# Second attention of a gated cross-attention stack: TensorE turns two heads and then scores two heads, where it did one of each in turn

## The chip, the cores and the metric

The kernel runs on one core of one Trainium2 chip. The metric is device time of one execution in microseconds (us); the time of a kernel is the median of several executions. The profile is one more execution, with the hardware profiler on. In its rows PE is TensorE's matmul side, PEld its loading of weights (the stationary operand), DVE is VectorE, ACT is ScalarE, POOL is GpSimd, and SPq the queue in which SyncE issues DMAs.

## The reference

Four blocks follow each other on x (16 batches, 112 tokens, 512 wide) with a context of 375 tokens a batch: an attention, a feed-forward, a second cross-attention, and a last block with causal attention. Only the third is touched:

```
q = (hidden_states @ Wq).reshape(B, S, 16, 128)          # B = 16, S = 112
k = (encoder_hidden_states @ Wk).reshape(B, S_enc, 4, 128)  # S_enc = 375
v = (encoder_hidden_states @ Wv).reshape(B, S_enc, 4, 128)
q = rms_norm(q, q_norm_w); k = rms_norm(k, k_norm_w)
k = jnp.repeat(k, 4, axis=2); v = jnp.repeat(v, 4, axis=2)
scores = jnp.einsum('bqhd,bkhd->bhqk', q, k) * scale
probs = jax.nn.softmax(scores, axis=-1)
out = jnp.einsum('bhqk,bkhd->bqhd', probs, v)
return out.reshape(B, S, 16 * 128) @ Wo
```

## The kernel before

The program runs in stages one after another. The stage of this study is the one whose tiles begin with `c_`; q, k and v have been projected and lie in DRAM. It goes through the 16 batches, and in a batch through 16 heads, in groups of four heads (`HPG`) that share a key and value head (`G` = 4 groups). Each operand of a matmul is split into a high and a low part, and a product is three passes (high by high, low by high, high by low).

Each engine has its own program, written out by hand and run strictly in the written order; semaphores are the only link between them. In the list, h is the head, and a line number is that of the profile.

- `scores(h)` on PE, three matmuls into one of four banks (L1905). It waits until the bank has been read by the exponential of head h-4.
- `maximum(h)` on DVE reads the bank (L1835). `exps(h)` on ACT writes the probabilities, in a ring of four, and their sum (L1776). `reciprocal(h)` on DVE (L1839), `scale(h)` on POOL multiplies the probabilities by it (L1729).
- `turn(h)` on PE transposes the probabilities in three pieces (L1913) into one of two banks. It waits for `scale(h)`, and for `probs_lo(h-2)`, which is the last reader of its bank.
- `probs_hi(h)` on ACT (L1783) and then `probs_lo(h)` on DVE (L1845) take the turned bank out as high and low part.
- `weigh(g)` on PE, nine matmuls for the four heads of group g (L1923), and `out_hi` on ACT (L1787) and `out_lo` on DVE (L1849) that take its bank out; `project(g)` on PE, twelve matmuls with Wo (L1934).

The order within a head's step is a matter of the four bodies. PE at step h does `turn(h)`, `scores(h+4)`, and then, where the tables name h, a weighing or a projection. The tables give a weighing at steps 2, 6, 10 and 14 (`WEIGH`; the one at step 2 is group 3 of the batch before), and a projection at steps 0, 4, 8 and 12 (`PROJECT`). `SPLIT_OUT` puts `out_hi` and `out_lo` at steps 3, 7, 11 and 15, one step behind each weighing.

ACT at step 3, 7, 11 or 15 does `out_hi`, then `probs_hi(h)`, then `exps(h+3)`. DVE at the same step does `out_lo`, then `reciprocal(h+2)`, `maximum(h+4)`, `probs_lo(h)`. POOL at step h does `scale(h)`. Splits of the next batch's q, k and v stand between, at steps of their own tables.

The loop over batches (`batches`) runs a first body without a batch before it, fourteen in a hardware loop of two bodies, one without a batch after, and one that only finishes.

Of the kernel before, what the change touches and what calls it, by code (L numbers as in the profile page):

```python
# [29 lines left out]
H = 16  # L30
# [52 lines left out]
def batches(eng, head, body, count=B):  # L83


    head((0, 0, 0))
    body(None, (0, 0, 0), (1, 1, 0))
    with eng.Fori(0, count // 2 - 1) as i:
        body((2 * i, 0, i), (2 * i + 1, 1, i), (2 * i + 2, 0, i + 1))
        body((2 * i + 1, 1, i), (2 * i + 2, 0, i + 1), (2 * i + 3, 1, i + 1))  # L90
    last = count // 2 - 1
    body((count - 2, 0, last), (count - 1, 1, last), None)
    body((count - 1, 1, last), None, None)
# [1543 lines left out]
def phase_c_attention(nc, keep, io, wo):  # L1637
# [5 lines left out]
    AHEAD = 4  # L1643
# [4 lines left out]
    WEIGH = {2: -1, 6: 0, 10: 1, 14: 2}  # L1648
    SPLIT_OUT = {3: -1, 7: 0, 11: 1, 15: 2}
    PROJECT = {0: -2, 4: -1, 8: 0, 12: 1}  # L1650
# [6 lines left out]
    with Memory(nc, "c") as m:  # L1657
# [28 lines left out]
        def group(slots, h, before, cur):  # L1686

            if h not in slots:
                return None
            which = before if slots[h] < 0 else cur  # L1690
            return which and (*which, slots[h] % G)

        @block.sync
        def _(sp):
            def load(b, p, half):
                sp.dma_start(q_raw[:, :, :], io["q1"][:, :, bass.ds(b * S, S)]).then_inc(q_loaded, 16)
                sp.dma_start(k_raw[:, :, :], io["k1"][b, :, :, :]).then_inc(k_loaded, 16)

                sp.dma_start(v_raw[:, :, :], io["v1"][b, :, :, :]).then_inc(v_loaded, 16)

            def load_x(b, p, half):
                sp.dma_start(xin[:, p, :], io["x2"][b, :, :]).then_inc(x_loaded[p], 16)

            def head(cur):
                load(*cur)
                load_x(*cur)

            def body(before, cur, after):
                if after:
                    sp.wait_ge(q_split, G * cur[0] + G)  # L1710
                    sp.wait_ge(k_split, G * cur[0] + G)
                    sp.wait_ge(v_split, KC * cur[0] + KC)
                    load(*after)
                if before:
                    b, p, half = before
                    sp.wait_ge(x_done, b + 1 + 1)
                    sp.dma_start(io["x3"][b, :, :], xout[:, p, :]).then_inc(x_stored[p], 16)
                if after:
                    load_x(*after)

            batches(sp, head, body)
            for p in range(2):
                sp.wait_ge(x_stored[p], 16 * (B // 2) + 16)
# [170 lines left out]
        @block.tensor  # L1894
        def _(pe):
            pe.sem_inc(turned_ready, AHEAD)
            ident = keep["ident"]

            def scores(b, p, h):
                if h % HPG == 0:  # L1900
                    pe.wait_ge(q_split, G * b + h // HPG + 1)
                    pe.wait_ge(k_split, G * b + h // HPG + 1)
                pe.wait_ge(probs_ready, H * b + h + 1)
                for n, (s, r) in enumerate(PASSES):
                    last = pe.matmul(score[h % AHEAD][0:S, 0:TE], q[s][:, p, h, :], k[r][:, p, h // HPG, :],  # L1905
                                     start=n == 0, stop=n == len(PASSES) - 1)
                last.then_inc(scores_ready, 1)

            def turn(b, h):
                pe.wait_ge(scaled, H * b + h + 1)  # L1910
                pe.wait_ge(pT_split, H * b + h + 1)
                for c in range(KC):
                    last = pe.transpose(turned[h % 2][0:KP, c * S:(c + 1) * S], probs[:, h % AHEAD, c * KP:(c + 1) * KP], ident[0:S, 0:S])  # L1913
                last.then_inc(turned_ready, 1)

            def weigh(b, p, half, g):
                pe.wait_ge(pT_split, H * b + HPG * (g + 1) + 2)
                pe.wait_ge(o_split, G * b + g + 1)
                if g == 0:
                    pe.wait_ge(v_split, KC * b + KC)  # L1920
                for n, (s, r) in enumerate(PASSES):
                    for c in range(KC):
                        last = pe.matmul(outp[:, 0:HPG * S], v[s][:, p, c, g * P:(g + 1) * P],  # L1923
                                         pT[r][:, g % 2, c, :, :].rearrange("p j s -> p (j s)"),
                                         start=n == 0 and c == 0, stop=n == len(PASSES) - 1 and c == KC - 1)
                last.then_inc(out_ready, 1)

            def project(b, p, half, g):
                pe.wait_ge(o_split, G * b + g + 1 + 1)
                if g == 0:  # L1930
                    pe.wait_ge(x_done, b + 1)
                for n, (s, r) in enumerate(PASSES):
                    for j in range(HPG):
                        last = pe.matmul(y[0:S, :], oT[s][:, g % 2, j, :], wo[r][:, HPG * g + j, :],  # L1934
                                         start=g == 0 and n == 0 and j == 0, stop=g == G - 1 and n == len(PASSES) - 1 and j == HPG - 1)
                if g == G - 1:
                    last.then_inc(y_ready, 1)

            def body(before, cur, after):
                if cur and not before:  # L1940
                    for h in range(AHEAD):
                        scores(cur[0], cur[1], h)
                for h in range(H):
                    if cur:
                        turn(cur[0], h)
                    if cur and h + AHEAD < H:
                        scores(cur[0], cur[1], h + AHEAD)
                    elif after and h + AHEAD >= H:
                        scores(after[0], after[1], h + AHEAD - H)
                    done = group(WEIGH, h, before, cur)  # L1950
                    if done:
                        weigh(*done)
                    done = group(PROJECT, h, before, cur)
                    if done:
                        project(*done)

            batches(pe, lambda cur: None, body)


# [514 lines left out]
```

## Time and profile before

| what | value |
|---|---|
| median of 3 runs | 2183.25 us (2183.11 to 2185.81) |
| the profiled execution | 2183.04 us |
| its span, first to last instruction | 2181.3 us |
| PE busy | 2042.6 us, 94% of the span |
| DVE, ACT, POOL busy | 60%, 52%, 31% |
| mean granted TensorE clock | 0.971 of full speed |

The profiled execution lies 1.7 us above its span and 0.2 us below the median. The shares are means over stages of different character, so the stage of the change has to be read by itself; it lies between about 1337 and 1862 us of the span. A busy PE is not a PE at its peak: matmuls overlap, and the spacing of their starts tells what one costs, not its duration.

### The profile page before, as it was taken

The page shows a single profiled execution, that of the slowest core. Times are in us where ns is not written, and L with a number is a line of the kernel's source. Part 1 is how long each engine was busy: PE and PEld are TensorE (multiplying, and loading weights), DVE is VectorE, ACT ScalarE, POOL GpSimd, SP SyncE. Part 2 cuts the span into 40 slices and gives each one's busy share as a digit, 9 for nine tenths or more (in the row PEclk, how much of TensorE's full clock was granted, in tenths as well). Part 3 has the DMA queues.
Part 4 walks back from the last instruction along what each step waited for, and adds up shares of the span by engine and source line. Part 5 has one row for each costly group of instructions (what it writes and reads, how often), then busy time and mean ns, then how long its engine had stood idle before and what let it go on. Part 6 is the DMA issues. An engine that isn't in the chain of part 4 may idle for free. (4 is left out here: it accounts for less than half of the span.)

```text
span 2181.3 us, 38580 instructions
## 1 busy us (share of the span) xinstructions
PE 2042.6 (94%) x13464; PEld 1691.5 (78%) x13464; DVE 1316.7 (60%) x2603; ACT 1139.9 (52%) x3025; POOL 666.3 (31%) x814
## 2 busy tenths in 40 slices
PE   5999999999989999999969995999999999689997
PEld 4777777777768888898848884888888888578884
DVE  5666667666644543564345554777777776466664
ACT  4666666666643333443323435677667665245453
POOL 2424425345311000000014443554555554012221
PEclk9999999999999999999979997999999999799997
DMA  5435436344265210100033344322322320311010
GB/s 151 151 97 151 146 96 212 117 145 136 92 201 191 76 58 1 68 4 27 0 121 116 116 120 137 100 71 98 103 92 72 107 98 13 109 50 43 28 34 26
DMA packets 167398, 205.96 MB, mean 94 GB/s; under 512 B 63680, under 2 KB 105664, under 8 KB 166752
## 3 DMA queue, kind: packets, MB, share of 16 engines
q1 hardware_dynamic: 167264, 204.15, 29.8%
q8 instruction: 87, 1.43, 0.3%
q14 instruction: 47, 0.39, 0.1%
HBM read 128.13 MB, written 75.99 MB: 94 GB/s over the span
## 5 line engine op out<-in xcount | busy, mean ns | idle before, releaser
L1729 POOL TENSOR_TENSOR c_probs<-c_probs,c_rsum 112x375 f32<-112x375 f32 x256 | 213.1, 835 | 231.1 <-DVE c_rsum L1839 225.3
L1835 DVE TENSOR_REDUCE c_nmax<-c_score 112x1 f32<-112x375 f32 x256 | 136.2, 533 | 97.4 <-PE c_score L1905 97.4
L1783 ACT ACTIVATE c_pT_hi<-c_turned 125x336 fp32r<-125x336 f32 x256 | 115.6, 452 | 107.9 <-PE c_turned L1913 107.9
L1224 ACT ACTIVATE b_silu<-b_gate,b_ug_scale 128x512 f32<-128x512 f32 (+1 forms) x64 | 40.7, 636 | 250.1 <-PE b_up L1330 250.0
L1281 DVE SCALAR_TENSOR_TENSOR b_hidden<-b_up,b_ug_scale,b_silu 128x512 f32<-128x512 f32 (+1 forms) x64 | 43.7, 683 | 204.8 <-ACT b_silu L1224 204.8
L547 ACT ACTIVATE a_probs<-a_score,a_nmax 112x375 f32<-112x375 f32 x256 | 144.7, 576 | 36.5 <-DVE a_nmax L707 36.5
L1776 ACT ACTIVATE c_probs<-c_score,c_nmax 112x375 f32<-112x375 f32 x256 | 148.2, 579 | 0.0
L918 PEld LDWEIGHTS a_turned<-keep_ident,a_probs 112*125 112x125 f32 x768 | 110.6, 189 | 47.0 <-issue 34.7
L918 PE MATMUL a_turned<-keep_ident,a_probs 112*125 112x112 f32 x768 | 135.1, 285 | 9.6 <-DVE a_pT L713 9.6
L1454 POOL TENSOR_TENSOR q_x_ve<-q_x_mv,keep_ln_eps 128x1 f32<-128x1 f32 x14 | 2.7, 192 | 444.8 <-DVE q_x_mv L1531 444.8
L2108 POOL TENSOR_TENSOR f_probs<-f_probs,f_rsum 112x448 f32<-112x448 f32 x64 | 60.3, 942 | 243.8 <-DVE f_rsum L2228 243.5
L2140 ACT ACTIVATE f_probs<-f_score,f_nmax 112x112 f32<-112x112 f32 x256 | 87.3, 353 | 90.4 <-DVE f_nmax L2223 89.6
L1913 PEld LDWEIGHTS c_turned<-keep_ident,c_probs 112*125 112x125 f32 x768 | 121.8, 189 | 16.3 <-POOL c_probs L1729 7.4
L1845 DVE TENSOR_TENSOR c_pT_lo<-c_turned,c_pT_hi 125x336 fp32r<-125x336 f32 x256 | 127.1, 497 | 4.6 <-ACT c_pT_hi L1783 4.4
L1913 PE MATMUL c_turned<-keep_ident,c_probs 112*125 112x112 f32 x768 | 123.4, 269 | 6.0 <-POOL c_probs L1729 5.4
L707 DVE TENSOR_REDUCE a_nmax<-a_score 112x2 f32<-112x750 f32 x128 | 120.1, 938 | 4.4
L1905 PE MATMUL c_score<-c_k_hi,c_q_hi 128*112 128x376 f32 x256 | 104.6, 409 | 16.4 <-DVE c_q_lo L1822 16.4
L704 DVE COPY_PREDICATED a_score<-keep_later,a_score 112x224 f32<-112x224 uint8 x128 | 49.7, 388 | 82.0 <-PE a_score L876 82.0
L1500 ACT ACTIVATE q_squares<-q_q_bank 128x512 f32<-128x512 f32 x56 | 33.5, 598 | 118.5 <-PE q_q_bank L1610 118.5
L555 ACT ACTIVATE a_pT<-a_turned 125x336 f32<-125x336 f32 x128 | 57.8, 452 | 68.9 <-PE a_turned L918 66.8
L1342 PE MATMUL b_y<-b_wd_hi,b_hT_hi 128*128 128x512 f32 x224 | 87.8, 392 | 1.9 <-DVE b_hT_lo L1286 1.9
L466 POOL TENSOR_TENSOR a_ssq_eps<-a_ssq,keep_rms_eps 125x4 f32<-125x4 f32 x48 | 9.8, 203 | 258.3 <-DVE a_ssq L717 258.3
(306 smaller groups left out, 5986.7 us busy)
## 6 DMA issues: line engine op xcount, KB each, us to landing
q<-q_qT SPq DMA_DIRECT2D x14, 1024.0 KB
c_q_raw<-q SPq DMA_DIRECT2D x16, 896.0 KB
k<-ab_stage SPq DMA_DIRECT2D x16, 752.0 KB, 4.3
c_k_raw<-k SPq DMA_DIRECT2D x16, 752.0 KB
v<-ab_stage SPq DMA_DIRECT2D x48, 250.0 KB
c_v_raw<-v SPq DMA_DIRECT2D x16, 750.0 KB
ab_lead<-in_ctx_dram SPq DMA_DIRECT2D x16, 672.0 KB
wug<-a_ug_turned SPq DMA_DIRECT2D x32, 256.0 KB, 2.4
```

Source lines behind the costliest of these rows:

```text
L547: last = act.activation(probs[:, n % RING, i, :], score[0:S, h % HPG, 0:T], ACT.Exp, bias=nmax[:, b % 2, h:h + 1], accum_out=sums[:, b % 2 ...
L707: dve.tensor_reduce(nmax[:, b % 2, 2 * n:2 * n + 2], score[0:S, pair, 0:T], axis=AX.X, op=ALU.max, negate=True).then_inc(max_done, 1)
L918: last = pe.transpose(turned[0:KP, c * S:(c + 1) * S], probs[:, n % RING, i, c * KP:(c + 1) * KP], ident[0:S, 0:S])
L1342: last = pe.matmul(y[b][:, :], hT[s][:, p, b * P:(b + 1) * P], wd[r][:, p, :], start=c == 0 and k == 0, stop=c == IC - 1 and k == len(PASS ...
L1729: pool.tensor_tensor(probs[:, h % AHEAD, :], probs[:, h % AHEAD, :], rsum[:, p, h:h + 1].broadcast_to([S, T]), ALU.mult).then_inc(scaled, 1)
L1776: act.activation(probs[:, h % AHEAD, :], score[h % AHEAD][0:S, 0:T], ACT.Exp, bias=nmax[:, p, h:h + 1], accum_out=sums[:, p, h:h + 1]).the ...
L1783: act.activation(pT[0][:, g % 2, :, j, :], src, ACT.Copy).then_inc(pT_hi, 1)
L1835: dve.tensor_reduce(nmax[:, p, h:h + 1], score[h % AHEAD][0:S, 0:T], axis=AX.X, op=ALU.max, negate=True).then_inc(max_done, 1)
L1845: dve.tensor_tensor(pT[1][:, g % 2, :, j, :], src, f32(pT[0][:, g % 2, :, j, :]), ALU.subtract).then_inc(pT_split, 1)
L1905: last = pe.matmul(score[h % AHEAD][0:S, 0:TE], q[s][:, p, h, :], k[r][:, p, h // HPG, :], start=n == 0, stop=n == len(PASSES) - 1)
L1913: last = pe.transpose(turned[h % 2][0:KP, c * S:(c + 1) * S], probs[:, h % AHEAD, c * KP:(c + 1) * KP], ident[0:S, 0:S])
L2140: last = act.activation(probs[:, t % RING, j, :], score[0:S, SETS * (t % SETS) + a, half * S:(half + 1) * S], ACT.Exp, bias=nmax[:, t % RI ...
```

## The change

The PE body of the stage goes through the heads in pairs: two turns, two scores, and then what the tables name for either head. No other engine's program is touched, no instruction is added or removed, and no wait is changed.

```
-                for h in range(H):
-                    if cur:
-                        turn(cur[0], h)
-                    if cur and h + AHEAD < H:
-                        scores(cur[0], cur[1], h + AHEAD)
-                    elif after and h + AHEAD >= H:
-                        scores(after[0], after[1], h + AHEAD - H)
-                    done = group(WEIGH, h, before, cur)
-                    if done:
-                        weigh(*done)
-                    done = group(PROJECT, h, before, cur)
-                    if done:
-                        project(*done)
+
+                for first in range(0, H, 2):
+                    for h in (first, first + 1):
+                        if cur:
+                            turn(cur[0], h)
+                    for h in (first, first + 1):
+                        if cur and h + AHEAD < H:
+                            scores(cur[0], cur[1], h + AHEAD)
+                        elif after and h + AHEAD >= H:
+                            scores(after[0], after[1], h + AHEAD - H)
+                    for h in (first, first + 1):
+                        done = group(WEIGH, h, before, cur)
+                        if done:
+                            weigh(*done)
+                        done = group(PROJECT, h, before, cur)
+                        if done:
+                            project(*done)
```

PE before, from the weighing at step 2 (or 6, 10, 14) to the next projection; `c_turned1` is the bank of the odd head 3, `c_turned0` that of head 4, `c_score3` and `c_score0` those of heads 7 and 8:

```order
L1923 MATMUL c_outp<-c_pT_hi,c_v_hi 128x448 x3
L1923 MATMUL c_outp<-c_pT_lo,c_v_hi 128x448 x3
L1923 MATMUL c_outp<-c_pT_hi,c_v_lo 128x448 x3
L1913 MATMUL c_turned1<-keep_ident,c_probs 125x112 x3
L1905 MATMUL c_score3<-c_k_hi,c_q_hi 112x376
L1905 MATMUL c_score3<-c_k_lo,c_q_hi 112x376
L1905 MATMUL c_score3<-c_k_hi,c_q_lo 112x376
L1913 MATMUL c_turned0<-keep_ident,c_probs 125x112 x3
L1905 MATMUL c_score0<-c_k_hi,c_q_hi 112x376
L1905 MATMUL c_score0<-c_k_lo,c_q_hi 112x376
L1905 MATMUL c_score0<-c_k_hi,c_q_lo 112x376
L1934 MATMUL c_y<-o_wo_hi,c_oT_hi 112x512 x4
```

Behind the weighing stood the turn of head 3, and the turn of head 5 comes only after the projection.

PE with the change, at the same place, from the weighing to the next projection; the banks are those of heads 4 and 5 for the turns, and of heads 8 and 9 for the scores:

```order
L1923 MATMUL c_outp<-c_pT_hi,c_v_hi 128x448 x3
L1923 MATMUL c_outp<-c_pT_lo,c_v_hi 128x448 x3
L1923 MATMUL c_outp<-c_pT_hi,c_v_lo 128x448 x3
L1913 MATMUL c_turned0<-keep_ident,c_probs 125x112 x3
L1913 MATMUL c_turned1<-keep_ident,c_probs 125x112 x3
L1905 MATMUL c_score0<-c_k_hi,c_q_hi 112x376
L1905 MATMUL c_score0<-c_k_lo,c_q_hi 112x376
L1905 MATMUL c_score0<-c_k_hi,c_q_lo 112x376
L1905 MATMUL c_score1<-c_k_hi,c_q_hi 112x376
L1905 MATMUL c_score1<-c_k_lo,c_q_hi 112x376
L1905 MATMUL c_score1<-c_k_hi,c_q_lo 112x376
L1934 MATMUL c_y<-o_wo_hi,c_oT_hi 112x512 x4
```

The turn of head 3 has moved ahead of the weighing, and the turn of head 5 has moved to the second place behind it.

DVE at step 3 (or 7, 11, 15), the same before and with the change; `c_oT_lo` is `out_lo`, `c_rsum` the reciprocal of head 5, `c_nmax` the maximum of head 7, `c_pT_lo` is `probs_lo` of head 3:

```order
L1849 TENSOR_TENSOR c_oT_lo<-c_outp,c_oT_hi 128x448
L1838 REGISTER_ALU
L1839 RECIPROCAL c_rsum<-c_sums 112x1
L1835 TENSOR_REDUCE c_nmax<-c_score 112x1
L1845 TENSOR_TENSOR c_pT_lo<-c_turned,c_pT_hi 125x3x112
```

Nothing moved here, and the orders of ACT, POOL and SyncE are the same too.

## Rows read from the trace of the kernel before

**Rows 1.** Windows: stretch, busy us (instructions) of PE, PEld, DVE, ACT, POOL, granted clock, DMA.

```profile
1350.00:1820.00 470.00, 469.48 (x2664) 419.77 (x2663) 349.71 (x923) 330.96 (x942) 254.63 (x284) 1.00 0.27 91
```

**Rows 2.** Waits between 1350 and 1820: who waited for whom, us, times, longest.

```profile
ACT c_oT_hi L1787 <- PE c_outp L1923: 41.7, 59, 1.3
...
PE c_turned L1913 <- DVE c_pT_lo L1845: 0.5, 2, 0.3
```

**Rows 3.** Timeline of PE around one weighing (start, us, engine, instruction).

```profile
1560.42 0.40 PE L1905 MATMUL c_score<-c_k_hi,c_q_hi 128*112 128x376 f32 x1
1560.66 0.33 PE L1905 MATMUL c_score<-c_k_lo,c_q_hi 128*112 128x376 f32 x1
...
1561.00 0.48 PE L1913 MATMUL c_turned<-keep_ident,c_probs 112*125 112x112 f32 x3
1561.25 0.40 PE L1905 MATMUL c_score<-c_k_hi,c_q_hi 128*112 128x376 f32 x1
...
1561.83 0.78 PE L1923 MATMUL c_outp<-c_pT_hi,c_v_hi 125*128 125x448 f32 x3
...
1563.67 0.48 PE L1913 MATMUL c_turned<-keep_ident,c_probs 112*125 112x112 f32 x3
...
1565.34 1.09 PE L1934 MATMUL c_y<-o_wo_hi,c_oT_hi 128*112 128x512 f32 x4
...
1568.11 0.48 PE L1913 MATMUL c_turned<-keep_ident,c_probs 112*125 112x112 f32 x3
...
1569.77 0.57 PE L1923 MATMUL c_outp<-c_pT_hi,c_v_hi 125*128 125x448 f32 x2
```

**Rows 4.** The same timeline, ACT, DVE and POOL behind that weighing (idle before, releaser).

```profile
1563.87 0.55 ACT L1787 ACTIVATE c_oT_hi<-c_outp 128x448 fp32r<-128x448 f32 x1 [0.41 <-PE c_outp L1923]
...
1564.44 0.62 DVE L1849 TENSOR_TENSOR c_oT_lo<-c_outp,c_oT_hi 128x448 fp32r<-128x448 f32 x1
...
1564.98 0.15 DVE L1839 RECIPROCAL c_rsum<-c_sums 112x1 f32<-112x1 f32 x1
1565.05 0.53 DVE L1835 TENSOR_REDUCE c_nmax<-c_score 112x1 f32<-112x375 f32 x1
...
1565.22 2.67 POOL L1729 TENSOR_TENSOR c_probs<-c_probs,c_rsum 112x375 f32<-112x375 f32 x3 [1.33 <-DVE c_rsum L1839]
...
1565.50 0.50 DVE L1845 TENSOR_TENSOR c_pT_lo<-c_turned,c_pT_hi 125x336 fp32r<-125x336 f32 x1
```

**Rows 5.** One line, `scale`: ns of one, shortest, median, longest.

```profile
L1729 POOL TENSOR_TENSOR c_probs<-c_probs,c_rsum x256: 808/813/1201, 1345.8 to 1844.9; 112x375 f32<-112x375 f32 x128
```

**Rows 6.** Timeline of the stage's start: a turn that waited.

```profile
1350.56 0.49 DVE L1845 TENSOR_TENSOR c_pT_lo<-c_turned,c_pT_hi 125x336 fp32r<-125x336 f32 x1
...
1351.20 0.55 PE L1913 MATMUL c_turned<-keep_ident,c_probs 112*125 112x112 f32 x3 [0.32 <-DVE c_pT_lo L1845]
...
1351.52 0.40 PE L1905 MATMUL c_score<-c_k_hi,c_q_hi 128*112 128x376 f32 x1
```

**Rows 7.** Timeline of PE in two earlier stages, around idle stretches.

```profile
910.35 0.50 PE L1342 MATMUL b_y<-b_wd_hi,b_hT_hi 128*128 128x512 f32 x1 [1.62 <-DVE b_hT_lo L1286]
...
1129.05 1.09 PE L1610 MATMUL q_q_bank<-q_w_lo,q_xT_hi 128*128 128x512 f32 x4
1129.98 1.09 PE L1610 MATMUL q_q_bank<-q_w_hi,q_xT_lo 128*128 128x512 f32 x4
...
1134.22 1.63 PE L1610 MATMUL q_q_bank<-q_w_hi,q_xT_hi 128*128 128x512 f32 x4 [2.71 <-DVE q_w_lo L1551]
...
1138.66 0.60 PE L1619 MATMUL q_t_bank<-keep_ident,q_qn 128*128 128x128 f32 x4
```

**Rows 8.** Windows around those idle stretches (the last three numbers: granted clock, DMA).

```profile
905.00:916.00 11.00, 9.32 (x63) 8.18 (x62) 9.34 (x16) 4.39 (x8) 0.00 (x0) 1.00 0.40 143
1128.00:1131.00 3.00, 3.00 (x15) 2.37 (x14) 1.14 (x2) 2.40 (x2) 1.30 (x3) 1.00 0.00 0
1134.80:1138.10 3.30, 3.30 (x9) 2.65 (x8) 1.93 (x3) 0.00 (x0) 1.22 (x2) 0.50 0.00 0
```

## The prediction

> **What bounds the kernel now.** I read the windows first. Between 1350 and 1820 us, most of the stage, PE is busy for 469.48 of 470.00 us at full clock, while DVE is busy for 349.71, ACT for 330.96 and POOL for 254.63 [rows 1]. So PE sets the pace, and every wait given to PE goes into the time in full, unless PE's own work shrinks. The waits agree: ACT's `out_hi` alone waits 41.7 us for PE, and PE waits twice in all, for 0.5 us [rows 2]. There is next to no PE idle time that a new order could remove. What is left for it to win is the spacing of matmuls; what it can lose is waits.
>
> The PE timeline gives the pattern. From the start of one weighing, at 1561.83, to the next, at 1569.77, is 7.94 us: four heads, one weighing of 1.84 us (1561.83 to 1563.67) and one projection of 2.77 us (1565.34 to 1568.11) [rows 3]. That is about 31.8 us a batch.
>
> **The change, part by part.** No instruction is added, so the PE work stays as it is, except for spacing.
>
> *Spacing, a gain.* The first score matmul behind a turn holds PE for 0.24 us (1560.42 to 1560.66), the next two for 0.17 us each (both to 1561.00) [rows 3]. A turn costs 0.25 us (1561.00 to 1561.25). In a pair the second head's first score follows a score and not a turn, so I let it cost 0.17: a gain of 0.07 us. Of 256 heads' scores, four are issued ahead of the first step, which leaves 252, or 126 pairs: 126 x 0.07 = 8.8 us. The lower bound is nothing, if the extra belongs to the switch of banks and not to the turn ahead of it. For two turns in a row I take 0.25 each.
>
> The Trainium skill (TensorE: Matmul & The Clock Gate, section "Back-to-back issue gap") gives the isolated gap between matmuls as their columns divided by 2.4 GHz plus 2.5 ns, which for 376 columns is 159 ns whatever ran before. The trace agrees for the second and third pass (0.17) and not for the first (0.24). By the page there would be no spacing to win, and the sum below would be 8.8 us higher.
>
> *A wait, the main term.* Call W the moment at which PE goes on behind a weighing, 1563.67 in the rows. What hangs on that weighing, through engines that keep their written order, is seen in one place [rows 4]:
>
> - ACT's `out_hi` waited for the weighing and starts at 1563.87 (W+0.20); `probs_hi(3)` stands behind it.
> - DVE's `out_lo` starts at 1564.44 (W+0.77). Behind it stand the reciprocal of head 5 at 1564.98, the maximum of head 7 at 1565.05, and `probs_lo(3)` at 1565.50 for 0.50, which ends at 1566.00 (W+2.33).
> - POOL's `scale(5)` starts at 1565.22, 0.09 behind the end of that reciprocal, and one takes 0.813 us [rows 5]: it ends at 1566.03 (W+2.36).
>
> `turn(5)` needs both `scale(5)` and `probs_lo(3)`. Before, it stands behind the projection, at 1568.11 (W+4.44) [rows 3], so 2.1 us of slack cover the chain. With the change it is the second thing behind the weighing: `turn(4)` takes PE from W to W+0.25, and then `turn(5)` waits. `turn(3)` and `scores(7)` have moved ahead of the weighing, so nothing of the chain starts later, but nothing starts earlier either: `out_hi` waits for the weighing as before, and `probs_hi(3)`, whose turn is now long done, stays behind it on ACT. `out_lo` likewise holds up the reciprocal and `probs_lo(3)` on DVE.
>
> When does PE go on? A turn that waited for `probs_lo` started 0.15 us behind its end (1350.56 + 0.49 = 1351.05, turn at 1351.20), and held PE for 0.32 instead of 0.25 (1351.20 to 1351.52) [rows 6]. So `turn(5)` starts at W+2.48 and costs 0.07 more: 2.48 - 0.25 + 0.07 = 2.30 us lost. By the POOL end alone, with no delay at all, it would be 2.36 - 0.25 = 2.11. I take 2.30, and 2.0 to 2.5 as bounds.
>
> Queued behind the waiting turn are `scores(8)`, `scores(9)` and the projection. Their readers, `maximum(8)` and `maximum(9)`, get their banks later, but the 2.77 us projection [rows 3] then covers maximum, `probs_lo` and `scale` for heads 6 and 7 (0.53 + 0.50 on DVE, 0.81 on POOL [rows 4, 5]). So the pair behind the projection should not wait. The pair ahead of the weighing is covered in the same way by that weighing of 1.84 us: `probs_lo(2)` needs a maximum of 0.53 and its own 0.50.
>
> How often: there are 64 weighings. Batch 0 has three (at heads 6, 10, 14), batches 1 to 15 have four each, and the closing body has one with no turn behind it; the one at head 14 of the last batch is followed by no turn either. 62 x 2.30 = 142.6 us.
>
> *The start.* Up to head 7 of batch 0 no weighing or projection covers anything, and PE waits for the chain of a single head already (0.32 in [rows 6]). Pairs make this chain somewhat longer; I put 2 us, with 0 to 6 as bounds.
>
> *The clock.* In the stall PE lies idle from the end of `turn(4)` (0.48 long, W+0.48) to W+2.48, some 2.0 us. Around an idle stretch of 1.62 us (ended at 910.35) the granted clock stays 1.00; after one of 2.71 us (ended at 1134.22) it is 0.50, the 1.2 GHz level [rows 7, 8]. The price of a fall shows there: twelve matmuls took 4.44 us (1134.22 to 1138.66, where PE goes on to other work), while four of the same shape take 0.93 at full clock (1129.05 to 1129.98), so twelve 2.79: 1.65 us lost a fall [rows 7, 8]. Idle of 2.0 us lies between the two rows, somewhat nearer to the one that kept the clock. I take a fall at one stall in six, 10 x 1.65 = 16.5 us; the ends are none and 62 x 1.65 = 102 us.
>
> *Sum.* -8.8 + 142.6 + 2 + 16.5 = +152.3 us. The profiled execution took 2183.04 us, which is 0.2 under the median of the runs, so nothing has to be corrected: 2335 us.
>
> **The rivals.**
>
> *The clock falls in nearly every stall.* For it: 2.71 us of idle time cost the clock, and 2.0 is not far below. Against it: 1.62 did not [rows 7, 8], and the stall is followed and preceded by dense work. It would give 2335 - 16.5 + 102 = 2421 us; halfway, 2370. The Trainium skill (TensorE: Matmul & The Clock Gate, Part 1) says that the slow level is the default and that activity is what lifts it; the two rows agree, and no row here shows 2.0 us.
>
> *The chain behind the weighing is shorter than it looks*, for instance because ACT and DVE come to it with less work in their queues. The engines would have to be late at W because of older work; but `out_hi` shows 0.41 us of idle time ahead of it [rows 4], and over the stage it waits 41.7 us for the weighing [rows 2]. Half a stall would give 2335 - 71 - 16.5 = some 2248 us.
>
> *Faster.* If `turn(5)` found `scale(5)` and `probs_lo(3)` done at W+0.25, only the spacing would be left: 2183.0 - 8.8 = 2174 us. This decides at 0.07 us a group of four heads: two pairs win 0.14, so a stall under 0.14 us a group would already leave a gain. For it speaks only that PE had no waits in this stage until now [rows 2]. Against it stands the order: both must come behind `out_lo` on DVE, which cannot start before the weighing has ended.
>
> That the change does nothing is excluded by the order of PE's instructions, which has the pairs as written.
>
> **How the numbers follow.** Stalls with few falls of the clock: 0.75, at 2335 us, by itself 2300 (2.0 us a stall, no fall: 2183 - 8.8 + 124 + 2) to 2375. The clock falling at more than half of them: 0.15. A much shorter chain: 0.06. Faster: 0.03. No difference: 0.01. The range from 2300 to 2395 leaves out the most extreme clock case and the short chains. What a measurement of this kernel can tell from no change is about 0.2%, or 4.4 us. Slower therefore has 0.96, faster 0.03, the same 0.01.
>
> **What would show it.** In the changed kernel's waits, PE or PEld at L1913 should wait 62 times for `c_probs` of POOL or `c_pT_lo` of DVE, some 2.0 us each, about 125 us in all. The stage's PE share should fall from 1.00 to about 0.8, and from weighing to weighing there should be some 10.1 us instead of 7.94, a little more where the clock falls. Every second first pass of `c_score` should hold PE for 0.17 us. ACT, DVE and POOL should have the same busy times. The prediction is wrong if turns behind projections wait too, if the stall is covered, or if the granted clock in the stage lies well under 0.95 (many falls).

## The result, and the profile after

The changed kernel takes 2331.47 us (median of 4 runs, 2329.29 to 2336.56) against 2183.59 for the kernel before (4 runs): a ratio of 1.0678, with a 95% interval of 1.066 to 1.0697. That is 147.9 us slower, where +152 us (2335 us) was forecast. The profiled execution is the longest of the four, 2336.56 us with a span of 2334.8; the others are 5.0 to 7.3 us shorter, with a mean granted clock of 0.970 to 0.971 of full speed against its 0.967.

The windows of the kernel after, as in [rows 1] (busy us of PE, PEld, DVE, ACT, POOL, then granted clock and DMA), for the stage's start, for most of the stage, and for a stretch in it that is slower:

```profile
1346.50:1363.30 16.80, 15.71 (x51) 13.22 (x52) 7.33 (x21) 7.95 (x23) 6.37 (x8) 0.50 0.49 161
1366.00:2000.00 634.00, 509.89 (x2769) 448.92 (x2770) 396.80 (x966) 346.32 (x963) 257.92 (x293) 0.99 0.19 65
1458.90:1494.50 35.60, 29.24 (x135) 25.46 (x136) 18.35 (x47) 16.31 (x47) 12.20 (x15) 0.86 0.25 82
```

PE was busy all the time; now it is busy for 509.89 of 634.00 us, 0.80. The waits of PE in that stretch are one line:

```profile
PE c_turned L1913 <- POOL c_probs L1729: 125.0, 62, 2.2
```

62 waits and 125 us, both as forecast. The timeline of the kernel after around one of them (start, us, what; in brackets the idle time ahead of it and its releaser), with all engines:

```profile
1593.65 0.77 PE L1923 MATMUL c_outp<-c_pT_hi,c_v_lo 125*128 125x448 f32 x3
...
1594.26 0.48 PE L1913 MATMUL c_turned<-keep_ident,c_probs 112*125 112x112 f32 x3
1594.46 0.54 ACT L1787 ACTIVATE c_oT_hi<-c_outp 128x448 fp32r<-128x448 f32 x1 [2.19 <-PE c_outp L1923]
...
1595.04 0.62 DVE L1849 TENSOR_TENSOR c_oT_lo<-c_outp,c_oT_hi 128x448 fp32r<-128x448 f32 x1 [1.43 <-ACT c_oT_hi L1787]
...
1595.58 0.15 DVE L1839 RECIPROCAL c_rsum<-c_sums 112x1 f32<-112x1 f32 x1
1595.65 0.53 DVE L1835 TENSOR_REDUCE c_nmax<-c_score 112x1 f32<-112x375 f32 x1
...
1595.81 1.74 POOL L1729 TENSOR_TENSOR c_probs<-c_probs,c_rsum 112x375 f32<-112x375 f32 x2 [3.08 <-DVE c_rsum L1839]
1596.09 0.50 DVE L1845 TENSOR_TENSOR c_pT_lo<-c_turned,c_pT_hi 125x336 fp32r<-125x336 f32 x1
...
1596.73 0.55 PE L1913 MATMUL c_turned<-keep_ident,c_probs 112*125 112x112 f32 x3 [2.00 <-POOL c_probs L1729]
...
1597.05 0.41 PE L1905 MATMUL c_score<-c_k_hi,c_q_hi 128*112 128x376 f32 x1
```

With W = 1594.26, `out_lo` starts at W+0.78, the reciprocal at W+1.32, `probs_lo` ends at W+2.33, and the second turn starts at W+2.47. The same chain stood in [rows 4] at W+0.77, W+1.31 and W+2.33. It is not longer than before; it is now waited for. The turn holds PE for 0.32 us, so a stall costs 2.47 - 0.25 + 0.07 = 2.29 us.

### The profile page after: what moved, and what is told of

Its sections match the earlier page's. It is cut to its first block and busy times, and to the rows that moved or that the text cites. A ratio compares the mean times of both kernels' runs of the same rounds, so it can differ in the third digit from the quotient of the medians.

```text
span 2334.8 us, 38580 instructions
## 1 busy us (share of the span) xinstructions
PE 2071.5 (89%) x13464; PEld 1708.9 (73%) x13464; DVE 1353.8 (58%) x2603; ACT 1147.5 (49%) x3025; POOL 659.2 (28%) x814
## 3 DMA queue, kind: packets, MB, share of 16 engines
q8 instruction: 87, 1.43, 0.2%
## 5 line engine op out<-in xcount | busy, mean ns | idle before, releaser
L1729 POOL TENSOR_TENSOR c_probs<-c_probs,c_rsum 112x375 f32<-112x375 f32 x256 | 207.5, 811 | 389.0 <-DVE c_rsum L1839 381.3
L1913 PEld LDWEIGHTS c_turned<-keep_ident,c_probs 112*125 112x125 f32 x768 | 111.2, 192 | 152.1 <-POOL c_probs L1729 141.3
L1905 PE MATMUL c_score<-c_k_hi,c_q_hi 128*112 128x376 f32 x256 | 98.3, 384 | 16.7 <-DVE c_q_lo L1822 16.7
L1787 ACT ACTIVATE c_oT_hi<-c_outp 128x448 fp32r<-128x448 f32 x64 | 34.8, 543 | 132.3 <-PE c_outp L1923 132.3
L1849 DVE TENSOR_TENSOR c_oT_lo<-c_outp,c_oT_hi 128x448 fp32r<-128x448 f32 x64 | 40.0, 625 | 92.5 <-ACT c_oT_hi L1787 92.5
```

The lines of the kernel that those rows point to most:

```text
L1729: pool.tensor_tensor(probs[:, h % AHEAD, :], probs[:, h % AHEAD, :], rsum[:, p, h:h + 1].broadcast_to([S, T]), ALU.mult).then_inc(scaled, 1)
```

## The experiments

The theory: the chain from a weighing through `out_hi` and `out_lo` holds the second turn behind it. The main rival: pairs as such are too much for two turned banks. All but the fifth start from the changed kernel. Where a time is one execution, it carries the scatter that the four runs above show.

**Out of the weighing one step later.** `out_hi` and `out_lo` go to the step behind, so that nothing of heads 3 and 5 stands behind them.

```
-    SPLIT_OUT = {3: -1, 7: 0, 11: 1, 15: 2}
+    SPLIT_OUT = {0: -2, 4: -1, 8: 0, 12: 1}
```

> Pairs as in the change, but out_hi and out_lo one step later (at steps 4, 8, 12 and 0), so that probs_hi(3), the reciprocal of head 5, the maximum of head 7 and probs_lo(3) no longer stand behind them. Theory (the stall is the chain from the weighing through out_hi and out_lo): the 62 waits of 2.0 us at the second turn shrink to a few tenths, 2185 to 2205 us. Rival (pairs as such are too much for two turned banks and four rings): the stalls stay, above 2310 us.

Measured: 2210.68 us (one execution), against 2181.93 for the kernel before on the same chip. The waits of PE:

```profile
PE c_turned L1913 <- POOL c_probs L1729: 13.3, 15, 0.9
PE c_y L1934 <- DVE c_oT_lo L1849: 1.9, 2, 1.3
```

Of 62 waits 15 are left, one a batch, and short ones. With the pairs in place and only the table moved, some 121 us came back: pairs as such are not what stalls. The time is 6 us above what was expected. The walk had missed the one step of a batch in which DVE finishes the batch before (the output and its statistics, 1.43 us of DVE) ahead of a reciprocal. Of the 29 us that still separate this run from the kernel before, 4.3 stand at the start (12.9 us from the first turn to the first weighing, against 8.6).

**Pairs shifted by one head.**

```
-                for first in range(0, H, 2):
-                    for h in (first, first + 1):
+                for heads in ((0,), *((n, n + 1) for n in range(1, H - 1, 2)), (H - 1,)):
+                    for h in heads:
...
```

The other two inner loops of the body run over `heads` too.

> Pairs are heads 1 and 2, 3 and 4, to 13 and 14, with 0 and 15 alone; tables as they were. The weighing at step 2 now comes behind the pair that ends with head 2, and turn(5) again behind the projection (W+4.4 us). Theory: no stall, the time of the kernel before to within 0.4%, 2178 to 2192 us; two turns in a row cost 0.58 instead of 0.50 us in the profile of the change, which eats the 0.07 us that two scores in a row win, so no gain either. Rival (pairs as such): still above 2310 us.

Measured: 2192.82 us (4 runs), a ratio to the kernel before of 1.0044 (1.0027 to 1.0061); a miss by 1 us at the upper end. Turns are paired, scores are paired, and the 62 stalls are gone, because a weighing is now followed by the turns of heads 3 and 4, and the turn of head 5 comes behind the projection. What is left is small and in sight. The timeline, once behind a weighing and once behind a projection:

```profile
1561.84 0.50 DVE L1845 TENSOR_TENSOR c_pT_lo<-c_turned,c_pT_hi 125x336 fp32r<-125x336 f32 x1
...
1562.07 0.97 PE L1913 MATMUL c_turned<-keep_ident,c_probs 112*125 112x112 f32 x6
...
1562.81 0.40 PE L1905 MATMUL c_score<-c_k_hi,c_q_hi 128*112 128x376 f32 x1
...
1566.69 0.81 PE L1913 MATMUL c_turned<-keep_ident,c_probs 112*125 112x112 f32 x6
1567.26 0.41 PE L1905 MATMUL c_score<-c_k_hi,c_q_hi 128*112 128x376 f32 x1
```

Two turns hold PE for 0.57 us behind the projection and for 0.74 behind the weighing, where the second of them waits for a `probs_lo` that ends at 1562.34. A wait of 0.17 us inside a pair does not appear in the list of waits. It comes in some groups only: from weighing to weighing two of the four groups of a batch take 7.9 to 8.0 us, as in the kernel before, and the other two 8.1 and 8.3. Over the stage, from the first weighing to the last, that makes 7.5 us (505.1 against 497.6), and the stage's start another 3.0 (11.6 us from the first turn to the first weighing, against 8.6).

**`out_lo` last in DVE's step.**

```
                 for h in range(H):
-                    done = group(SPLIT_OUT, h, before, cur)
-                    if done:
-                        out_lo(*done)
                     if cur:
                         ahead(reciprocal, h + RECIPROCAL)
                         ahead(maximum, h + AHEAD)
                         probs_lo(cur[0], h)
+                    done = group(SPLIT_OUT, h, before, cur)
+                    if done:
+                        out_lo(*done)
```

> Pairs as in the change; on DVE out_lo goes behind reciprocal, maximum and probs_lo of its step, ACT keeps out_hi first. Theory: probs_lo(3) then waits for probs_hi(3) alone, which stands behind out_hi on ACT and ends at W+1.1; it ends at W+1.6, turn(5) starts at W+1.75, and a stall of 2.29 becomes about 1.55: 62 x 0.74 = 46 us off, about 2285 us. Rival 1 (only scale on POOL, the releaser that the profile names, holds the turn): its reciprocal is early now, so about 2190 us. Rival 2 (out_lo has no part): 2331 us.

Measured: 2288.04 us (one execution). PE waits:

```profile
PE c_turned L1913 <- DVE c_pT_lo L1845: 79.9, 61, 1.5
```

Each wait shrinks from 2.0 to 1.3 us, and the time by 43 us. So DVE's order is about a third of the stall. What holds the rest can be read in this trace, around one weighing:

```profile
1591.35 0.48 PE L1913 MATMUL c_turned<-keep_ident,c_probs 112*125 112x112 f32 x3
1591.54 0.55 ACT L1787 ACTIVATE c_oT_hi<-c_outp 128x448 fp32r<-128x448 f32 x1 [1.75 <-PE c_outp L1923]
...
1591.98 0.44 ACT L1783 ACTIVATE c_pT_hi<-c_turned 125x336 fp32r<-125x336 f32 x1
...
1592.46 0.51 DVE L1845 TENSOR_TENSOR c_pT_lo<-c_turned,c_pT_hi 125x336 fp32r<-125x336 f32 x1 [0.32 <-ACT c_pT_hi L1783]
```

With W = 1591.35, `out_hi` starts at W+0.19 and `probs_hi(3)` right behind it on ACT at W+0.63; DVE lies idle until that is done, and `probs_lo(3)` ends at W+1.62, where W+1.6 was expected. No run moved `out_hi` alone.

**Only the reciprocal ahead of `out_lo`.** The others keep their order.

```
                 for h in range(H):
+                    if cur:
+                        ahead(reciprocal, h + RECIPROCAL)
                     done = group(SPLIT_OUT, h, before, cur)
                     if done:
                         out_lo(*done)
                     if cur:
-                        ahead(reciprocal, h + RECIPROCAL)
                         ahead(maximum, h + AHEAD)
```

> Pairs as in the change; on DVE only the reciprocal goes ahead of out_lo, so scale(5) is done before W. Theory: probs_lo(3) ends at W+2.33 behind out_lo and the maximum all the same, so the wait changes its releaser from POOL to DVE and shrinks by no more than 0.1 us: 2322 to 2332 us. Rival (POOL, which the profile names, is the cause): the stall goes, about 2190 us.

Measured: 2329.65 us (one execution). PE waits (L1914 is the turn, moved by a line):

```profile
PE c_turned L1914 <- DVE c_pT_lo L1845: 119.3, 61, 2.2
```

POOL, the only releaser named in the profile of the change, is out of the list, and the time is the same within the scatter: `probs_lo` on DVE had ended only 0.03 us ahead of `scale` all along (W+2.33 and W+2.36, by [rows 4, 5]), and holds the turn almost as long by itself. A releaser is the last of several, not the cause.

**The kernel before, with the outputs one step later.** The table edit of the first experiment, on single heads in turn.

> The kernel before, single heads in turn, with out_hi and out_lo one step later. Theory (what matters is what stands ahead of what in each engine's order): turn(3) comes behind the weighing here, so probs_hi(3), exps(6) and probs_lo(3) run ahead of out_hi and out_lo, out_lo ends at about W+2.8 while PE reaches the projection at W+1.7, and 64 projections wait 1.1 to 2 us: 2250 to 2310 us. Rival (a later out_hi and out_lo is better in any order): 2183 us or less.

Measured: 2279.39 us (one execution), 96 us slower than the kernel before. PE waits:

```profile
PE c_y L1934 <- DVE c_oT_lo L1849: 77.7, 62, 2.0
```

The same edit that gives 121 us to the paired order takes 96 from the single one, and the wait moves to the projection. Neither table nor order is good by itself.

**The weighing between turns and scores.**

```
                     for h in (first, first + 1):
                         if cur:
                             turn(cur[0], h)
+                    for h in (first, first + 1):
+                        done = group(WEIGH, h, before, cur)
+                        if done:
+                            weigh(*done)
                     for h in (first, first + 1):
                         if cur and h + AHEAD < H:
                             scores(cur[0], cur[1], h + AHEAD)
...
                     for h in (first, first + 1):
-                        done = group(WEIGH, h, before, cur)
-                        if done:
-                            weigh(*done)
                         done = group(PROJECT, h, before, cur)
```

> Pairs as in the change, but the weighing stands between the two turns and the two scores, so that 1.1 us of scores follow it ahead of the next turns. By slack alone (stall minus the work put behind the weighing): 2.29 - 1.1 = 1.2 us, about 2260 us. Theory with the written order of DVE: the maximum of head 6 and probs_lo(2) stand ahead of out_lo, and wait for scores that now come behind the weighing, so turn(4) waits too (some 0.7 us) and the chain to turn(5) starts later by as much; nothing is won, 2320 to 2370 us.

Measured: 2384.99 us (one execution), 15 us above the upper end. The waits of PE, and the window of the stage:

```profile
PE c_turned L1913 <- POOL c_probs L1729: 93.6, 61, 2.4
PE c_turned L1913 <- DVE c_pT_lo L1845: 38.6, 61, 0.6
```

```profile
1366.00:2035.00 669.00, 538.33 (x2693) 453.89 (x2692) 383.02 (x942) 353.10 (x939) 249.05 (x285) 0.95 0.19 62
```

The mechanism is the expected one: both turns behind a weighing wait, 132 us together, and the 1.1 us of scores put ahead of them won nothing, since they delay a maximum that stands ahead of `out_lo` on DVE. What was not expected is the clock, at 0.95 of full speed against 0.99. It goes together with the step that the walk had missed in the first experiment, in which DVE finishes the batch before. Here that work stands ahead of `out_lo`:

```profile
1537.17 0.55 DVE L1835 TENSOR_REDUCE c_nmax<-c_score 112x1 f32<-112x375 f32 x1 [3.87 <-PE c_score L1905]
...
1538.05 0.74 DVE L1856 SCALAR_TENSOR_TENSOR c_xout<-c_y,keep_gates,c_xin 112x512 f32<-112x512 f32 x1
...
1538.94 0.69 DVE L1859 BATCH_NORM_STATS2 keep_bn<-c_xout 112x512 f32 x1
1539.55 0.61 DVE L1849 TENSOR_TENSOR c_oT_lo<-c_outp,c_oT_hi 128x448 fp32r<-128x448 f32 x1
...
1541.23 0.67 PE L1913 MATMUL c_turned<-keep_ident,c_probs 112*125 112x112 f32 x3 [2.40 <-POOL c_probs L1729]
```

The window behind that turn:

```profile
1541.50:1545.00 3.50, 3.50 (x13) 3.07 (x12) 2.31 (x8) 2.26 (x6) 1.35 (x2) 0.51 0.01 5
```

The second turn waits 2.40 us there, where 1.37 is usual in this run, and the clock falls. From weighing to weighing such a group takes 13.0 us or more, in 14 of the 16 batches; most other groups take 10.0 to 10.7. By an estimate, a mean of 0.95 is a tenth of the stretch, some 67 us, at the half level, which loses up to 33 us, 28 more than in the changed kernel. With 7 us of added waits that explains some 35 of the 54 us between the two; the rest is not traced.

**Single heads in batch 0, pairs from batch 1 on.**

```
-                for first in range(0, H, 2):
+                for heads in ([(n, n + 1) for n in range(0, H, 2)] if before else [(n,) for n in range(H)]):
...
```

The three inner loops run over `heads`.

> Pairs as in the change from batch 1 on, single heads in turn in batch 0. The profile of the change reaches the first weighing 7 us later than that of the kernel before, with the clock at its half level until 1363 us instead of 1350. Theory: those 7 us, and the 2 stalls of batch 0 (4.6 us), come back: about 2320 us. Rival (the slow clock at the start has another cause): about 2327 us, for the two stalls alone.

Measured: 2321.43 us (one execution), 10.0 below the median of the change, where 7 and 4.6 were expected together. The window of its start:

```profile
1344.00:1356.00 12.00, 10.40 (x55) 9.20 (x56) 7.59 (x23) 8.49 (x27) 7.41 (x10) 0.82 0.65 209
```

Its PE timeline, the first turn and the first weighing:

```profile
1345.07 0.97 PE L1913 MATMUL c_turned<-keep_ident,c_probs 112*125 112x112 f32 x3 [5.07 <-POOL c_probs L1729]
...
1353.66 0.78 PE L1923 MATMUL c_outp<-c_pT_hi,c_v_hi 125*128 125x448 f32 x3
```

The same two in the changed kernel:

```profile
1346.52 1.74 PE L1913 MATMUL c_turned<-keep_ident,c_probs 112*125 112x112 f32 x6 [5.22 <-POOL c_probs L1729]
...
1362.29 1.25 PE L1923 MATMUL c_outp<-c_pT_hi,c_v_hi 125*128 125x448 f32 x3
```

And in the kernel before:

```profile
1346.68 0.97 PE L1913 MATMUL c_turned<-keep_ident,c_probs 112*125 112x112 f32 x3 [5.45 <-POOL c_probs L1729]
...
1355.25 0.78 PE L1923 MATMUL c_outp<-c_pT_hi,c_v_hi 125*128 125x448 f32 x3
```

From the first turn to the first weighing it is 8.6 us with single heads, here and in the kernel before, and 15.8 in the changed kernel. There the whole start runs at 1.2 GHz (0.50 over 16.8 us, in the windows shown with the result); with single heads the clock comes up within it. But pairs alone do not hold the clock down. The fourth experiment has the same order of work up to the first weighing (a line further down), and its clock was up in time:

```profile
1346.25 1.74 PE L1914 MATMUL c_turned<-keep_ident,c_probs 112*125 112x112 f32 x6 [5.35 <-POOL c_probs L1729]
...
1359.17 0.77 PE L1924 MATMUL c_outp<-c_pT_hi,c_v_hi 125*128 125x448 f32 x3
```

```profile
1352.00:1358.00 6.00, 3.51 (x21) 2.62 (x20) 4.39 (x13) 4.17 (x14) 2.68 (x4) 1.00 0.41 149
```

It takes 12.9 us, as the first experiment does. So 4.3 us of the start come with the pairs, and 2.9 with the late clock of the changed kernel's profiled execution. The two stalls and those 4.3 us make 8.9, as near to the 10.0 measured as the 11.6 expected; one execution does not tell them apart.

**Scores in a row, turns apart.** Shifted pairs, but the second turn behind the scores. The loops as they stand after the edit, cut to what matters:

```
...
                     for h in heads[:1]:
                         if cur:
                             turn(cur[0], h)
                     for h in heads:
                         ...
                             scores(cur[0], cur[1], h + AHEAD)
                     for h in heads[1:]:
                         if cur:
                             turn(cur[0], h)
```

> Pairs 1 and 2 to 13 and 14, but in the order turn, two scores, turn, then the weighing or projection, so that scores stand in a row and turns do not; 0 and 15 alone. No stall by the theory: turn(5) comes behind the projection. Two scores in a row win 0.07 us in each of 112 pairs, 7.8 us, if a weighing or projection behind a turn costs no more than behind a score: 2175 us. If whatever follows a turn pays the 0.07 us, nothing is left: 2183 us. Slower than 2190 us would mean a wait that the walk through the orders has missed.

Measured: 2183.72 us (11 runs), against 2183.20 (15 runs); the ratio is 1.0001 (0.9992 to 1.001). No waits, no gain. Its PE timeline says why:

```profile
1560.30 0.34 PE L1905 MATMUL c_score<-c_k_hi,c_q_hi 128*112 128x376 f32 x1
1560.47 0.33 PE L1905 MATMUL c_score<-c_k_lo,c_q_hi 128*112 128x376 f32 x1
...
1560.81 0.48 PE L1913 MATMUL c_turned<-keep_ident,c_probs 112*125 112x112 f32 x3
1561.06 0.85 PE L1923 MATMUL c_outp<-c_pT_hi,c_v_hi 125*128 125x448 f32 x3
1561.75 0.78 PE L1923 MATMUL c_outp<-c_pT_lo,c_v_hi 125*128 125x448 f32 x3
1562.37 0.77 PE L1923 MATMUL c_outp<-c_pT_hi,c_v_lo 125*128 125x448 f32 x3
```

The first pass of the second head (1560.30) holds PE for 0.17 us, as forecast. But the first three matmuls of the weighing behind a turn now hold it for 0.69 where the next three hold it for 0.62: the 0.07 us is paid by whatever follows a turn. It is not the switch of banks that costs it, since the second head's scores go into another bank too. No order tried here is faster than the kernel before.

## Why the prediction was right

- **The wait, 142.6 us.** Right in place, count and size: 62 waits, 2.29 us each by the timeline (2.30 forecast), 142.0 us. That the chain through `out_hi` and `out_lo` is the cause is shown by the first and third experiments (take it away, or shorten it on DVE), and that pairs as such are not, by the first and second.
- **The releaser.** The prediction let the turn start 0.15 us behind the end of `probs_lo` (W+2.33, so W+2.48), though it had the end of `scale` 0.03 us later (W+2.36); the profile names POOL, and the turn starts at W+2.47. The fourth experiment shows that either of the two holds the turn almost equally long.
- **Spacing, -8.8 us.** Half right. The second head's first score costs 0.17. But "for two turns in a row I take 0.25 each" was wrong: two turns hold PE for 0.57. In a group of two pairs, one with its turns apart because of the stall, that leaves -0.07 - 0.07 + 0.07 = -0.07 us, some -4 us over 62 groups. So the rival *Faster* would have needed a stall under 0.07 us a group; its text gives that figure and, from 0.25 for each turn, 0.14.
- **The clock, +16.5 us.** Mis-sized: three falls, not ten, by the timeline of the change. From stall to stall it is 11.9, 11.8 and 11.7 us there, where 10.2 is usual (1586.50 to 1596.73, say). The fourth and seventh experiments, with nearly as many stalls, have three and two such long groups. The three of the changed kernel:

```profile
1459.05 0.94 PE L1913 MATMUL c_turned<-keep_ident,c_probs 112*125 112x112 f32 x3 [2.00 <-POOL c_probs L1729]
...
1470.98 0.58 PE L1913 MATMUL c_turned<-keep_ident,c_probs 112*125 112x112 f32 x3 [2.24 <-POOL c_probs L1729]
...
1482.78 0.93 PE L1913 MATMUL c_turned<-keep_ident,c_probs 112*125 112x112 f32 x3 [2.00 <-POOL c_probs L1729]
...
1494.52 0.55 PE L1913 MATMUL c_turned<-keep_ident,c_probs 112*125 112x112 f32 x3 [2.00 <-POOL c_probs L1729]
```

  The price of a fall (1.65) was right: 5 us for three.
- **The start, +2 us.** Mis-sized: 7.2 us in the changed kernel's profile, beyond its own bound of 6. The pairs bring 4.3 of it, within the bounds, as the first and fourth experiments show. The other 2.9 are the clock, which stays at its half level for the whole start in that execution and which this term of the prediction left out. Why it came up late there, with the same order of work, is open.
- **The busy times.** One sign did not come: DVE is busy for 1353.8 us over the program, where it was 1316.7. Of these 37 us, 31 lie in the splits of q and k (L1822 and L1826: 901 and 827 ns each on the mean, 642 and 598 before). They do not lengthen the chain, as DVE is idle for 1.43 us ahead of `out_lo` in the timeline shown with the result.
- **The sum.** 142.0 - 4 + 5 + 7.2 = 150 us by the changed kernel's profiled execution. From the first turn to the last weighing its stage is 153.0 us longer than before (1346.52 to 2005.61, against 1346.68 to 1852.80); its whole time is 153.5 us longer. The missing 3 us are about what a longer wait once a batch makes: in most batches one group of four takes 10.4 us from weighing to weighing, and its turn waits 2.19 us and not 2.00. The errors in spacing, clock and start largely cancelled, which is luck; the main term is not. The last weighing, before and with the change:

```profile
1852.80 0.78 PE L1923 MATMUL c_outp<-c_pT_hi,c_v_hi 125*128 125x448 f32 x3
```

```profile
2005.61 0.78 PE L1923 MATMUL c_outp<-c_pT_hi,c_v_hi 125*128 125x448 f32 x3
```

## What to carry to other kernels

An order written for one engine is half of a schedule: the tables that say where the other engines take results out were fitted to the place of the matmuls, and moving the matmuls alone put a 2.3 us chain, hidden until then, onto the engine that sets the pace. To see it beforehand, take one bank that is waited for, write down what stands ahead of its reader on each in-order engine, and measure that chain in the old trace, where it was already as long here, since nothing of it started later with the change. And a releaser named in a list of waits is the last to arrive: if another arrived 0.03 us ahead of it, removing the last brings next to nothing.

## What the runs showed of the hardware

- A turn costs 0.07 us more than its own 0.25, and what follows pays it: a score's first pass (0.24 instead of 0.17), three matmuls of a weighing (0.69 instead of 0.62), or another turn (0.57 for two). Grouping like with like only moves it.
- Idle stretches of 2.0 to 2.2 us, 62 times in one stage, cost the granted clock three times and left it alone 59 times. In the sixth experiment a wait of 0.6 us stands shortly ahead of a longer one. Where the longer one was 2.40 us, the clock fell to 0.51 behind it, and the group of heads is as long in 14 of 16 batches. Where it was 1.37 us, most groups kept the clock; behind one that ended at 1507.76 us it was 0.53. So the length of a single gap does not decide it.
- The same order of work met the clock differently: at the stage's start it was at full speed by 1352 us in the fourth experiment and at its half level until 1363 in the changed kernel, which made 2.9 us.
